# Counted loops and register arithmetic of a recurrent-plus-attention kernel written out with constant counts

## The chip, the cores and the metric

One core of one Trainium2 chip runs the kernel as one program. The metric is the device time of one execution in microseconds (us). The core has five engines that run their own instruction streams and meet at semaphores: TensorE (PE in the rows, its weight loads PEld), VectorE (DVE), ScalarE (ACT), GpSimd (POOL) and SyncE (SP), which here only issues DMAs. Each engine has a sequencer, which does register arithmetic, branches and semaphore waits and hands the rest to the engine.

## The reference, cut to what matters

```python
x = L0_attn_x                              # (16, 256, 128) float32
xn = _layernorm(x)
s = mamba_like(xn)      # W_in, two depthwise convs of 4 taps, silu; x_dbl = xs @ W_xdbl;
                        # delta = softplus(dt_low @ W_dt + 2*inv_dt); h = exp(delta*A)*h + delta*u*B (16 states);
                        # y = sum(h*C) + u*D; concat(y, z) @ W_out + b_out
g = silu(transformer(xn))
return x + s * g

# transformer: six layers of
x = attn_layer(shift_tokens(x), Wqkv, q_scale, k_scale, Wo) + x   # 16 heads of 64, q and k l2-normed,
                                                                  # rotary, causal window of 32
x = ffn_layer(shift_tokens(x), ln_g, ln_b, W1, b1, W2, b2) + x    # layer norm, a * gelu(gate) @ W2
```

## The kernel before, in words

The 16 sequences of 256 tokens form 8 groups of 512 tokens (`GT`). The kernel runs in four stages. First a layer norm of all tokens and the transposes to `xT` (channels on partitions). Then the state space stage (`state_groups`): for each of the 8 groups, 16 states; PE spreads B and C over the partitions, ACT makes the decays, DVE does the multiply and the scan (L1230, L1234), POOL weighs with C and adds (L1055, L1058).

The third and longest stage is the transformer (`flow`). Its unit of work is a turn, 48 of them with a current group. A turn carries four groups in different stages of a layer (`prev2`, `prev`, `cur`, `next`) and has 16 steps on each engine. In each step PE computes scores of a pair of heads (`scores`, L690, 16 matmul records a step), transposes probabilities (L699, L700), makes outputs (L718), and projects the next group's q and k (L335 to L337); DVE takes the maxima (L1338), multiplies by the rotary tables (L1292) and copies the transposed probabilities (L1324); ACT does the exponentials (L930); POOL normalises and rotates. The order within a step is fixed by hand-written tables. Four turns of a layer have an extra kind: in `load` and `T0` the next layer's weights are loaded and split in high and low parts and DVE makes new tables, `T1` and `T2` load the rest.

The last stage, eight small passes over the groups, takes silu on ACT (L1023), multiplies with the state space result on DVE (L1420), transposes on PE (L818) and adds x on DVE (L1424).

All engines run the same structure of loops. In `state_groups` groups 1 to 6 are a counted loop of three passes with two groups each. In `flow` the first three turns and the last ones are written with constants; between them a loop over five layers (L316) holds an inner loop `layer` of two passes with two turns each (L306) and then the four turns `load` to `T2`; the sixth layer has the inner loop alone. The last stage is a loop of eight passes. Each engine therefore takes a backward branch of L306 six times and one of L316 four times.

Where a count depends on a loop variable, the value of a wait is worked out in a register (`eng.snap`, `Bases`), `held` places the arithmetic ahead of the waits, and `settle` adds a wait on `consts_made`, a semaphore that has long been set. An instruction carries its waits itself as far as it can; other waits become semaphore instructions in front of it.

Of the kernel before, what the change touches and what calls it, by code (L numbers as in the profile page):

```python
# [19 lines left out]
GROUPS = TOKENS // GT  # L20
# [106 lines left out]
def build(nc, x_in, W_in, W_xdbl, W_dt, W_out, mvec, Wqkv, Wo, W1, W2, lvec, tabs_c, mask_c, ident_c,  # L127
          headsum_c, statepick_c, conv_w, out):
    ctx = ExitStack()
    with ctx:  # L130
# [169 lines left out]
        def flow(eng, turn, credited, plain=()):  # L300
# [15 lines left out]
            with eng.Fori(0, DEPTH - 1) as l:  # L316
                layer(l)
                for k, kind in enumerate(("load", "T0", "T1", "T2")):
                    turn(bases(eng.snap(l * GROUPS + (6 + k))), (-2, -1, 0, 1), k % 2,
# [19 lines left out]
        def after(eng, what, g, per, k):  # L339

            if not isinstance(g, int):
                eng.wait_ge(what, eng.snap(g * per + k))
            elif g * per + k > 0:
                eng.wait_ge(what, g * per + k)

        def state_groups(eng, group):

            group(0, 0, True)
            with eng.Fori(0, (GROUPS - 2) // 2) as h:
                group(eng.snap(h * 2 + 1), 1, True)  # L350
                group(eng.snap(h * 2 + 2), 0, True)
            group(GROUPS - 1, 1, False)

        def settle(eng):

            eng.wait_ge(consts_made, 1)
# [17 lines left out]
        def _(sp_e):  # L374
# [9 lines left out]
            def load_chunk(layer, c):  # L384

                done = sp_e.snap(layer * CHUNKS + (c - 1)) if not isinstance(layer, int) else layer * CHUNKS + c - 1
                if not isinstance(layer, int) or done > 0:
# [31 lines left out]
            with sp_e.Fori(0, GROUPS) as g:  # L419
# [6 lines left out]
            def turn(n, o, par, gs, kind, l):  # L426
# [3 lines left out]
                nl = l + 1 if isinstance(l, int) or kind not in ("load", "T0", "T1", "T2") else sp_e.snap(l + 1)  # L430

                def swap(j, q):

                    made = held(sp_e, n16 + (16 * q + j + 1))
# [4 lines left out]
                def keep_k_norms(h, q):  # L439

                    norms = held(sp_e, n2 + (2 * q + h + 1))
# [1058 lines left out]
```

## Time and profile before

| | us |
|---|---|
| median of 3 runs | 3862.33 (3861.29 to 3875.04) |
| profiled execution, its own time | 3852.33 |
| span of the profiled execution | 3850.5 |

The profiled execution lies 1.83 us above its span, and 10.0 us below the median of the three timed runs. It counts 107643 instructions, 31040 of them matmul records and as many weight loads. "busy" is time in which an engine works; register, branch and semaphore instructions do not count. The chain of waits is followed back from the last instruction: at each step to what released it, or to the instruction before it on its engine. "issue" in it is time in which the engine waited for nothing that the profile shows. The granted clock of TensorE is given as a share of full speed; full is 2.4 GHz and the other level, 1.2 GHz, is 0.5.

### The profile page before, as it was taken

The numbers are of one execution on the slowest core, as the hardware profiler recorded it, in microseconds if no ns is written. First come the engines' busy times: TensorE is split into PE (matmuls) and PEld (weight loads), VectorE is DVE, ScalarE is ACT, GpSimd is POOL, SyncE is SP. The second block draws the span as 40 slices with busy tenths as digits, with TensorE's granted clock in tenths as the row PEclk, the third lists the DMA queues.
The fourth block names the chain that finished last, engine by engine and source line by source line (L and its number), as shares of the span: only waits on it lengthen the run. The fifth ranks groups of instructions, "written<-read, shape, count | busy, mean of one in ns | idle before, by whom it ended". The sixth has DMA issues, their size and how long they took to land.

```text
span 3850.5 us, 107643 instructions
## 1 busy us (share of the span) xinstructions
PE 3513.4 (91%) x31040; PEld 2253.6 (59%) x31040; DVE 3251.6 (84%) x11659; ACT 3048.6 (79%) x8806; POOL 2918.7 (76%) x2417
## 2 busy tenths in 40 slices
PE   5998699999999999999999999999999999999994
PEld 2454466666666565666666666666656666666662
DVE  5778688889889888888888888888988988888882
ACT  4565588888878888888888887888877888888883
POOL 3888687778878778777788777787877877877771
PEclk9899799999999999999999999999999999999996
DMA  2000233323323233232233332333322333223222
GB/s 81 6 8 8 106 105 103 101 100 116 108 98 108 93 111 112 101 102 99 98 116 104 111 101 95 102 112 105 114 94 96 107 109 114 102 101 101 99 77 69
DMA packets 235888, 365.31 MB, mean 95 GB/s; under 512 B 43054, under 2 KB 75884, under 8 KB 235052
## 3 DMA queue, kind: packets, MB, share of 16 engines
q1 hardware_dynamic: 235276, 358.05, 27.5%
q8 instruction: 275, 4.51, 0.5%
q14 instruction: 337, 2.76, 0.2%
HBM read 125.93 MB, written 5.77 MB: 34 GB/s over the span
## 4 chain that ended last, share of the span: by engine, by line
PE 70%; DVE 14%; issue 6%; ACT 5%; POOL 2%; DMA 1%; SPq 1%; DVEq 0%; ACTq 0%; POOLq 0%
PE bank L729 9%; PE bank L335 8%; PE bank L718 8%; PE bank L690 8%; PE bank L337 7%; PE bank L336 6%; PE bank L671 5%; DVE ab L1292 4%; PE bank L699 4%; PE bank L757 4%; PE bank L700 3%; DVE sm L1338 3%; DVE pt L1324 2%; ACT L972 1%; PE bank L735 1%
## 5 line engine op out<-in xcount | busy, mean ns | idle before, releaser
L930 ACT ACTIVATE pr<-sm,nb,rq 128x128 f32<-128x128 f32 (+1 forms) x3072 | 1516.7, 500 | 22.5 <-DVE nb L1344 18.2
L1084 POOL TENSOR_TENSOR pr<-pr,rden 128x640 f32<-128x640 f32 x768 | 963.6, 1255 | 551.8 <-DVE rden L1317 550.2
L1292 DVE TENSOR_TENSOR ab<-bank,ltab 128x512 f32<-128x512 f32 x1536 | 985.5, 683 | 182.6 <-PE bank L337 161.0
L1092 POOL TENSOR_TENSOR rot<-ab,swp 128x512 f32<-128x512 f32 x768 | 984.2, 1281 | 97.7 <-DMA swp<-ab 92.0
L1338 DVE CUSTOM_DVE_ANT_0 sm<-bank,mask 128x128 f32<-128x128 f32 (+1 forms) x3072 | 840.3, 329 | 44.3 <-PE bank L690 35.3
L930 ACT ACTIVATION_READ_ACCUMULATOR pr<-sm,nb,rq 128x1 f32 x3072 | 595.3, 194 | 0.0
L690 PEld LDWEIGHTS bank<-rot 64*64 64x64 f32 x12288 | 291.0, 133 | 460.7 <-issue 460.1
L1098 POOL TENSOR_TENSOR rot<-rot,rkb 128x512 f32<-128x512 f32 x384 | 491.3, 1285 | 78.1 <-DMA rkb<-k_scratch 77.9
L1324 DVE COPY pt<-bank 128x512 f32<-128x512 f32 x768 | 531.4, 692 | 10.2
L918 ACT ACTIVATE sq<-bank 128x512 f32<-128x512 f32 x768 | 451.1, 587 | 94.8 <-DVE ab L1292 84.2
L690 PE MATMUL bank<-rot 64*64 64x96 f32 x12288 | 433.3, 256 | 87.6 <-issue 48.5
L718 PE MATMUL bank<-pt,vtok 128*64 128x160 f32 (+1 forms) x6144 | 464.1, 293 | 0.0
L699 PE MATMUL bank<-ident,pr 128*128 128x128 f32 x1536 | 399.4, 287 | 57.6 <-DVE pt L1324 55.6
L1338 DVE DVE_READ_ACCUMULATOR2_ANT bank<- 128x1 f32 x3072 | 432.2, 141 | 0.1
L939 ACT ACTIVATE wide<-bank 128x512 f32<-128x512 f32 x384 | 228.6, 595 | 247.9 <-PE bank L718 246.9
L718 PEld LDWEIGHTS bank<-pt,vtok 128*64 128x64 f32 x6144 | 370.7, 137 | 66.5 <-issue 66.1
L700 PE MATMUL bank<-ident,pr 128*128 128x128 f32 x1536 | 379.9, 274 | 0.0
L944 ACT ACTIVATE vtok<-bank 128x512 f32<-128x512 f32 x384 | 227.5, 592 | 183.6 <-PE bank L337 183.1
L729 PE MATMUL bank<-wide,wo 128*128 128x512 f32 x768 | 371.0, 606 | 0.9 <-ACT wide L939 0.9
L335 PE MATMUL bank<-xh,wqk_h 128*128 128x512 f32 x768 | 340.3, 443 | 27.0 <-ACT sq L918 25.8
L699 PEld LDWEIGHTS bank<-ident,pr 128*128 128x128 f32 x1536 | 216.4, 141 | 195.5 <-issue 156.9
L337 PE MATMUL bank<-xl,wqk_h 128*128 128x512 f32 x768 | 306.9, 400 | 0.0
(201 smaller groups left out, 6383.7 us busy)
## 6 DMA issues: line engine op xcount, KB each, us to landing
swp<-ab SPq DMA_DIRECT2D x1536, 128.0 KB, 2.0
rkb<-k_scratch SPq DMA_DIRECT2D x768, 128.0 KB, 2.9
xs<-xT SPq DMA_DIRECT2D x95, 128.0 KB, 2.3
xs<-xT SPq DMA_DIRECT2D x95, 127.5 KB, 2.4
raw<-Wqkv SPq DMA_DIRECT2D x48, 128.0 KB, 2.4
raw<-Wqkv SPq DMA_DIRECT2D x12, 256.0 KB, 2.7
wo<-Wo SPq DMA_DIRECT2D x6, 512.0 KB, 4.6
k_scratch<-rsum SPq DMA_DIRECT2D x192, 8.0 KB
```

Source lines behind the costliest of these rows:

```text
L335: eng.matmul(o, wh, ah, start=True, stop=False)
L337: return eng.matmul(o, wh, al, start=False, stop=True)
L690: mm = pe.matmul(bank[i][part, c:c + 96], rot[rows, p, c0 + 64 * half:c0 + 64 * half + 64], rot[rows, PAIRS + p, c0 + k0:c0 + k0 + 96], st ...
L699: pe.transpose(bank[2][:, 256 * i:256 * i + P], pr[:, e % 4, i, 0, 0:P], ident[:, :])
L718: mm = pe.matmul(bank[3][64 * i:64 * i + 64, cols], vtok[:, 2 * b + t, ch], pt[:, e % 4, i, t, 0:cols.stop - cols.start], start=(b == 0 an ...
L729: mm = pe.matmul(use_bank("wo", 0)[:, :], wo[:, p, :], wide[:, p, :], start=(p == 0), stop=(p == PAIRS - 1))
L930: ins = act.activation(pr[:, s % 4, i, t, 0:P + WINDOW * t], sm[:, s % 2, i, cs], ACT.Exp, bias=nb[:, s, t, i:i + 1], scale=head_scale(rq, ...
L1084: ins = pool.tensor_tensor(pr[:, e % 4, :, :, :], pr[:, e % 4, :, :, :], rden[:, e, :, :].rearrange("p t i -> p i t").unsqueeze(3) .to_bro ...
L1092: pool.tensor_tensor(rot[:, PAIRS * (j % 2) + j // 2, :], ab[:, j % 2, 0, :], swp[:, j % 2, :], ALU.add).then_inc(qk_rot, 1)
L1292: ins = dve.tensor_tensor(seqs(ab[:, j % 2, i, :]), seqs(use_bank("qk", j)[:, :]), ltab[:, 2 * (j % 2) + i:2 * (j % 2) + i + 1, :] .to_bro ...
L1324: dve.tensor_copy(pt[:, e % 4, :, :, 0:P], bank[2][:, :].rearrange("p (i t c) -> p i t c", i=2, t=2)).then_inc(p_Tsb, 1)
L1338: ins = dve.tensor_tensor_reduce(sm[:, s % 2, i, cs], bank[i][:, cs], mask[:, cs], 1.0, -3e38, ALU.add, ALU.max, mx[:, t, i:i + 1])
```

## The change

All counted loops are replaced by Python loops that write the turns, layers, groups and passes out, so every semaphore count, slice and layer number is a constant of the program. With that `held`, `settle`, the `snap` calls and all register instructions go. No engine operation of the turns and groups is changed or put in another order. The constants still form the same waits; those on `consts_made` that `settle` made are gone. PE's written program has 20272 matmul instructions where it had 5256.

```diff
-        def held(eng, n):
-
-            if not isinstance(n, int):
-                eng.to_reg(n)
-            return n
-
...
-                    self.n = {m: eng.snap(it * m + CREDIT) for m in credited}
-                    self.z = {m: eng.snap(it * m) for m in plain}
+                    self.n = {m: (it * m + CREDIT) for m in credited}
+                    self.z = {m: it * m for m in plain}
...
             def layer(l):
-                with eng.Fori(0, 2) as h:
-                    for k in range(2):
-                        g = eng.snap(h * 2 + k)
-                        it = eng.snap(h * 2 + (l * GROUPS + (2 + k)))
-                        turn(bases(it), (-2, -1, 0, 1), k, (g, eng.snap(g + 1), eng.snap(g + 4)),
-                             "first" if k == 0 else "", l)
+                for k in range(4):
+                    turn(bases(l * GROUPS + 2 + k), (-2, -1, 0, 1), k % 2, (k, k + 1, k + 4), "first" if k == 0 else "", l)
...
-            with eng.Fori(0, DEPTH - 1) as l:
+            for l in range(DEPTH - 1):
...
         def state_groups(eng, group):
 
             group(0, 0, True)
-            with eng.Fori(0, (GROUPS - 2) // 2) as h:
-                group(eng.snap(h * 2 + 1), 1, True)
-                group(eng.snap(h * 2 + 2), 0, True)
+            for g in range(1, GROUPS - 1):
+                group(g, g % 2, True)
             group(GROUPS - 1, 1, False)
-
-        def settle(eng):
-
-            eng.wait_ge(consts_made, 1)
...
                 def scores(s):
 
                     p, b = s // 2, s % 2
-                    scaled = held(pe, n8 + (p + 1))
-                    used = held(pe, n16 + s)
-                    settle(pe)
+                    scaled = (n8 + (p + 1))
+                    used = (n16 + s)
...
-            with act.Fori(0, GROUPS) as g:
+            for g in range(GROUPS):
...
                 def normalise(e, q):
-                    count = held(pool, n16 + (16 * q + e + 1))
-                    settle(pool)
+                    count = (n16 + (16 * q + e + 1))
```

The other hunks do the same in the other functions and engines.

On PE, at the end of the inner loop's second turn, this stood before (L690 are the scores that open the next turn, L335 to L337 the projections that close this one; ISA here is a fused register instruction):

```order
L335 MATMUL bank<-xh,wqk_h 128x512 [waits qk_sq]
L336 MATMUL bank<-xh,wqk_l 128x512
L337 MATMUL bank<-xl,wqk_h 128x512
L306 REGISTER_ALU
L306 COMPARE_AND_BRANCH
L279 ISA
L690 MATMUL bank<-rot 64x96 [waits sc_bias,k_norm,consts_made]
L690 MATMUL bank<-rot 64x96 x7
L625 ISA
L756 REGISTER_ALU [waits f_h]
L757 MATMUL bank<-gg,w 128x512 [waits f_h]
```

And this stands there in the changed program, where L325 to L327 are the projections, L671 the scores and L738 the down projection:

```order
L325 MATMUL bank<-xh,wqk_h 128x512 [waits qk_sq]
L326 MATMUL bank<-xh,wqk_l 128x512
L327 MATMUL bank<-xl,wqk_h 128x512
L671 MATMUL bank<-rot 64x96 [waits sc_bias,k_norm]
L671 MATMUL bank<-rot 64x96 x7
L738 MATMUL bank<-gg,w 128x512 [waits f_h]
```

The matmuls stand in the same order; the branch, the register instructions and the wait on `consts_made` between them are gone.

On ACT, in the last stage, the loop held a load of the silu table in each of its eight passes:

```order
L1022 REGISTER_ALU [waits f_add]
L1023 ISA [waits g_mul]
L1023 ACT_TABLE_LOAD
L1023 ACTIVATE ab<-xT 128x512
L1020 REGISTER_ALU
L1020 COMPARE_AND_BRANCH
```

Written out, the same place is:

```order
L1002 ACT_TABLE_LOAD [waits g_mul]
L1002 ACTIVATE ab<-xT 128x512 [waits f_add]
L1002 ACTIVATE ab<-xT 128x512 [waits g_mul,f_add] x7
```

The table is loaded once, and the other seven passes have the silu alone.

## Rows read from the trace of the kernel before

**Rows 1.** The page, busy time: us, share of the span, instructions

```profile
PE 3513.4 (91%) x31040; PEld 2253.6 (59%) x31040; DVE 3251.6 (84%) x11659; ACT 3048.6 (79%) x8806; POOL 2918.7 (76%) x2417
```

**Rows 2.** The page, TensorE's granted clock in tenths, 40 slices

```profile
PEclk9899799999999999999999999999999999999996
```

**Rows 3.** The page, chain that ended last, by engine

```profile
PE 70%; DVE 14%; issue 6%; ACT 5%; POOL 2%; DMA 1%; SPq 1%; DVEq 0%; ACTq 0%; POOLq 0%
```

**Rows 4.** Timeline of PE, scores that open turns: start, us, what [idle before]

```profile
560.00 0.54 PE L690 MATMUL bank<-rot 64*64 64x96 f32 x13
...
628.39 0.56 PE L690 MATMUL bank<-rot 64*64 64x96 f32 x16
...
699.85 0.69 PE L690 MATMUL bank<-rot 64*64 64x96 f32 x16 [3.02 <-issue]
...
770.12 0.56 PE L690 MATMUL bank<-rot 64*64 64x96 f32 x16
...
838.50 0.56 PE L690 MATMUL bank<-rot 64*64 64x96 f32 x16
...
909.05 0.56 PE L690 MATMUL bank<-rot 64*64 64x96 f32 x16 [0.39 <-DVE nb L1344]
...
979.33 0.56 PE L690 MATMUL bank<-rot 64*64 64x96 f32 x16
...
3641.32 0.56 PE L690 MATMUL bank<-rot 64*64 64x96 f32 x16
...
3709.86 0.56 PE L690 MATMUL bank<-rot 64*64 64x96 f32 x16
```

**Rows 5.** Chain in order of time, its long pieces of issue: start, us

```profile
696.84 3.02 issue
...
1676.72 3.58 issue
...
2381.72 2.92 issue
...
3499.69 2.98 issue
```

**Rows 6.** Sequencer instructions of L306 on PE: count, ns min/median/max, first and last start

```profile
L306 PEldq COMPARE_BRANCH  x12: 78/1694/3664, 696.0 to 3640.5; - x12
```

**Rows 7.** Timeline of DVE at the first backward branch of L306

```profile
695.47 0.16 DVE L1344 TENSOR_TENSOR nb<-bank,nrq 128x4 f32<-128x4 f32 x1
698.64 0.18 DVE L1317 RECIPROCAL rden<-den 128x4 f32<-128x4 f32 x1 [3.01 <-ACT pr L930]
```

**Rows 8.** Windows: stretch, length, busy of PE, PEld, DVE, ACT, POOL, clock, DMA

```profile
699.80:703.20 3.40, 3.35 (x22) 1.82 (x22) 3.21 (x13) 0.60 (x1) 1.64 (x2) 0.55 0.23 83
703.20:706.60 3.40, 3.40 (x36) 1.85 (x39) 1.88 (x4) 1.93 (x7) 3.32 (x3) 0.95 0.01 4
```

**Rows 9.** Windows of two groups of the state space stage

```profile
141.60:182.40 40.80, 37.18 (x105) 20.31 (x105) 31.54 (x36) 24.94 (x42) 32.74 (x27) 0.92 0.02 7
...
303.50:341.30 37.80, 34.19 (x106) 18.73 (x105) 31.30 (x35) 24.95 (x42) 32.86 (x27) 1.00 0.02 7
```

**Rows 10.** Timeline of one pass of the last stage

```profile
3831.14 1.28 ACT L1023 ACT_TABLE_LOAD   x1 [0.98 <-DVE ab L1420]
...
3831.17 1.11 PE L818 MATMUL bank<-ident,ab 128*128 128x128 f32 x4 [1.79 <-DVE ab L1420]
3832.42 0.69 DVE L1424 TENSOR_TENSOR rot<-rot,bank 128x512 f32 x1 [1.39 <-PE bank L818]
3832.44 0.63 ACT L1023 ACTIVATE ab<-xT 128x512 f32 x1
3833.23 0.69 DVE L1420 TENSOR_TENSOR ab<-ab,rot 128x512 f32<-128x512 f32 x1
```

**Rows 11.** The page, queues that fetch instructions: packets, MB, share

```profile
q8 instruction: 275, 4.51, 0.5%
q14 instruction: 337, 2.76, 0.2%
```

More of the change, by code:

```diff
@@ L339, in after @@
         def after(eng, what, g, per, k):
-            if not isinstance(g, int):
-                eng.wait_ge(what, eng.snap(g * per + k))
-            elif g * per + k > 0:
+            if g * per + k > 0:
                 eng.wait_ge(what, g * per + k)
@@ L429, in turn @@
                 nk, n2, n8, n16 = n.z[64], n.n[2], n.n[8], n.n[16]
-                nl = l + 1 if isinstance(l, int) or kind not in ("load", "T0", "T1", "T2") else sp_e.snap(l + 1)
+                nl = l + 1
                 def swap(j, q):
-                    made = held(sp_e, n16 + (16 * q + j + 1))
+                    made = (n16 + (16 * q + j + 1))
                     sp_e.wait_ge(qk_mul, made)
@@ L505, in _ @@
             ov = out.rearrange("b (t p) c -> p (b t) c", p=P)
-            with sp_e.Fori(0, GROUPS) as g:
+            for g in range(GROUPS):
                 sp_e.wait_ge(g_out, g + 1 + CREDIT)
@@ L573, in group @@
             def group(g, par, more):
-                before = g - 1 if isinstance(g, int) else pe.snap(g - 1)
-                following = g + 1 if isinstance(g, int) else pe.snap(g + 1)
-                if isinstance(g, int) and g == 0:
+                before = g - 1
+                following = g + 1
+                if g == 0:
                     spread_B(0, g, par)
@@ L812, in _ @@
             flow(pe, turn, (1, 2, 3, 4, 8, 16), (32,))
-            with pe.Fori(0, GROUPS) as g:
+            for g in range(GROUPS):
                 pe.wait_ge(g_mul, g + 1 + CREDIT)
@@ L874, in split_high @@
                 due = {0: 32, 2: 64, 4: 96, 6: 112, 1: 32, 3: 48, 5: 64, 7: 80}[c]
[L875 to L876 removed]
+                landed = total * layer + due
                 act.wait_ge(raw_in[c % 2], landed)
@@ L962, in split_high_x @@
                 def split_high_x(buf):
-                    landed = held(act, n.z[32] + 64 if cur is not None else n.z[32] + 32)
-                    settle(act)
+                    landed = (n.z[32] + 64 if cur is not None else n.z[32] + 32)
                     act.wait_ge(xs2_in, landed)
@@ L1018, in _ @@
             flow(act, turn, (1, 2, 3, 4, 8, 16), (32,))
-            with act.Fori(0, GROUPS) as g:
+            for g in range(GROUPS):
                 act.wait_ge(f_add, DEPTH * GROUPS + CREDIT)
@@ L1031, in split_low @@
             def split_low(layer, c):
-                made = held(pool, layer * CHUNKS + c + 1 if isinstance(layer, int) else pool.snap(layer * CHUNKS + (c + 1)))
-                settle(pool)
+                made = layer * CHUNKS + c + 1
                 pool.wait_ge(w_hi, made)
@@ L1101, in normed @@
                 def normed(q):
-                    ready = held(pool, n1 + (q + 1))
-                    vectors = held(pool, l + 2) if kind == "T2" else None
-                    settle(pool)
+                    ready = (n1 + (q + 1))
+                    vectors = (l + 2) if kind == "T2" else None
                     if vectors is not None:
@@ L1115, in split_low_x @@
                 def split_low_x(buf):
-                    made = held(pool, n1 + 3 if cur is not None else n1 + 2)
-                    settle(pool)
+                    made = (n1 + 3 if cur is not None else n1 + 2)
                     pool.wait_ge(x_hi, made)
@@ L1256, in layer_tables @@
                 ins.then_inc(lvq_ok, 1)
-                made = held(dve, base + 2)
-                settle(dve)
+                made = (base + 2)
                 dve.wait_ge(lvq_ok, made)
@@ L1329, in maxima @@
                     p, b = s // 2, s % 2
-                    scores = held(dve, n16 + (s + 1))
-                    used = held(dve, n16 + (s - 1 if s >= 2 or prev is not None else 0))
-                    settle(dve)
+                    scores = (n16 + (s + 1))
+                    used = (n16 + (s - 1 if s >= 2 or prev is not None else 0))
                     dve.wait_ge(sc_ps, scores)
@@ L1416, in _ @@
             dve.wait_ge(s_in, 32)
-            with dve.Fori(0, GROUPS) as g:
+            for g in range(GROUPS):
                 dve.wait_ge(g_silu, g + 1)
```

62 lines of the change are left out of this document (28 added, 34 removed).

## The prediction, made before the changed kernel ran

> **What bounds the kernel now.** I read the page first. PE works in 91% of the span, DVE in 84%, ACT in 79% [rows 1]; TensorE's clock is full in nearly all of the transformer [rows 2]; and the chain of waits is PE for 70%, DVE for 14%, with 6% of "issue" [rows 3]. So the transformer is bound by PE, with short pieces where DVE or ACT is late. What sequencers do counts only where it stops PE.
>
> To see that, the next view is the timeline of PE, cut at the scores that open each turn [rows 4]. A turn is a repeated unit with the same work, so its length is the measure. The turn from 560.00 lasts 68.39 us, the next, which ends with the inner loop's backward branch, 71.46 (699.85 minus 628.39), the one after it 70.27, and the next again 68.38. The row that opens the turn at 699.85 has 3.02 us of idle time put down to "issue": nothing that the profile shows was missing. The load turn lasts 70.55 and T0 70.28. The turn from 3641.32 is written with constants already in this kernel and is a full turn but for the load of a shifted input; it lasts 68.54.
>
> Then the chain in order of time. Its pieces of issue over 2.5 us in the transformer's loops are ten, of which four stand in [rows 5]; the smallest is 2.92, and all ten add up to 31.6. Ten is also the number of backward branches taken on each engine: six of L306, four of L316. The branch instruction itself takes between 78 ns and 3.66 us on PE [rows 6]. DVE shows the same hole at the same place, 695.63 to 698.64 [rows 7]. It is put down to ACT's exponentials there, but for each engine it is the start of the loop body again.
>
> After the hole the clock: 0.55 for the 3.4 us from 699.80, 0.95 in the next 3.4 [rows 8]. PE was idle for 3.0 us, then the chip granted it the lower level for 3.4 us, and this is what makes the following turn 70.27 where the undisturbed one is 68.38.
>
> **The change, part by part.** *Backward branches of the transformer.* Ten holes of 2.92 to 3.58 us go [rows 5]: 31.6 us. All engines have theirs within a few us of each other and wait for the same semaphores, so it is one hole a branch, not five. What is late next is PE itself: a turn that ends without a taken branch, such as the one from 560.00, goes on without a gap into the next [rows 4].
>
> *Clock after them.* Each restart at the lower clock costs up to 70.27 - 68.38 = 1.89 us [rows 4]. Ten of them would be 18.9; none is the lower bound, since the change does not say that the clock stays up. I can check the sum by the turns. The 44 turns from 560.00 to 3641.32 last 3081.3. If 34 turns take 68.39 and five pairs of load and T0 take 140.83 each (979.33 minus 838.50), that is 2325.3 + 704.2 = 3029.5, or 51.8 less. The later pairs may be longer than the first, and then this is too much. Between 31.6 and 51.8 I take 48: it is nearest to what the turns say, and it means 16.4 us for the clock.
>
> Here the Trainium skill bears on the case. Runtime: NRT & Kernel Launch, section Instruction fetch mechanics, says that prefetch is sequential and that a taken branch to a place outside two pages forces a fetch before execution goes on. The 3.0 us holes agree with it. The Trainium skill's page Advanced Engine Details and Errata, section Control Flow Timing, gives a compare-and-branch some 108 ns; by that figure the ten branches would be worth 1.1 us together (an estimate of that page), and this case's holes of 3.02 and 3.58 us say otherwise.
>
> *Register arithmetic, `held` and `settle` in the ordinary turns.* I cost this at nothing. The cover is that sequencers work ahead while their engines are busy. The test is the turn from 3641.32: it has no register arithmetic and lasts 68.54, against 68.39 with it [rows 4]. It still has the waits on `consts_made`, so those are unproved. Upper bound: 0.5 us a turn, about the 0.39 that PE waits for DVE at the scores at 909.05 [rows 4], or 22 for 44 turns; lower bound: the 0.15 between these two turns the other way, a loss of 7. I take 0, nearest to the constant turn.
>
> *Load and T0 turns.* They are 2.16 and 1.89 us longer than an ordinary one [rows 4], 20 us for five pairs. Most of it must be the work itself (splits on ACT and POOL, tables on DVE), which stays; a part is register work for slices and counts. Between 0 and 10 us I take 1.
>
> *State space stage.* It too has a loop with two backward branches. The group 141.60 to 182.40 lasts 40.8 at a mean clock of 0.92, the one from 303.50, in the same loop, 37.8 at 1.00 [rows 9]. So what differs between groups is the clock, 3.0 us a group; the four groups from 141.60 to 303.50 have a mean of 40.5. The change doesn't touch what precedes the clock's fall there, but shifts of a fraction of a us may move it. Between a loss of 6 and a gain of 13 I take 0.
>
> *Last stage.* A pass takes 2.89 us: silu's table load at 3831.14 (1.28), silu (0.63), the product at 3833.23 (0.69) and two short hand-overs. The load goes in seven passes, but 7 x 1.28 = 9.0 is not the gain. Beside it runs product, PE, sum, product: PE starts at 3831.17, the sum at 3832.42, it takes 0.69, and the next product starts at 3833.23 [rows 10]. That is 2.06 from PE's start to the product, 0.12 after the end of the sum, and with the product's 0.69 and the hand-over to PE again about 2.88. It becomes the bound in the load's place. It has three register instructions on its path of about 0.05 each: 0.1 to 0.2 a pass, 1 us for seven. If that cover weren't there, it would be 9.
>
> *Instruction fetch.* The new program is straight. The two queues moved 4.51 + 2.76 = 7.27 MB [rows 11], which over 107643 instructions is 67.5 bytes each, so already before every executed instruction is fetched about once per execution, loops or not. Without register instructions it should be slightly less. Cost 0, since the turns between two branches show no hole.
>
> Sum: 48 + 0 + 1 + 0 + 1 + 0 = 50. The profiled execution would go from 3852.3 to 3802; the median of the timed runs lies 10.0 higher, so 3862.3 - 50 = 3812.
>
> **Rivals.**
> 1. *More than the branches.* If waits on `consts_made` and register work are exposed after all, and the state space stage keeps its clock, the further gain is about 11 for ordinary turns (half of the 22), 5 in load and T0, and 9 of the 13: 25 together, 3787. For it: DVE and POOL have many such instructions. Against it: the constant turn is no faster.
> 2. *Holes go, clock does not.* PE loses time elsewhere at the lower level, or an engine that caught up in the hole is now late. Then only 31.6 + 1 goes, 3830. For it: the clock also fell in the state space stage, without a branch [rows 9]. Against it: turns that follow an unbranched end show nothing of the kind.
> 3. *No change.* The stall is not the branch but something at that point of the layer, such as queued DMAs. Then 1 or 2 us, 3861. Against it: the fall-through after the inner loop's second pass has no hole, at the same work (770.12 to 838.50 is 68.38).
> 4. *Slower: straight code outruns its fetch.* PE's queue brought 275 packets in the span, one in 14 us [rows 11]. If the next packet isn't always asked for ahead in a program of this length, PE stops for a hole of 3.1 us plus 1.9 at the low clock, 5.0 for each. It eats the gain at 10 such stops and makes the kernel slower by over 0.5% (19.3 us) from 14 on; one stop in ten packets would be 25, or 125 us: 3862 - 50 + 125 = 3937. For it: nothing in this trace is straight for longer than eight turns. Against it: within those turns dozens of packets pass without one hole.
>
> **How the numbers follow.** The forecast has 0.70, rival 1 0.12, rival 2 0.10, rival 3 0.04, rival 4 0.04. The time is the forecast's, 3812. The range takes in rivals 1 and 2 and the bounds of the state space stage beyond them by a little: 3785 to 3838; rivals 3 and 4 stay outside. A measurement of this kernel can tell about 0.5%, 19.3 us, from no change. Faster by more than that: the forecast and rivals 1 and 2, 0.92; within it rival 3 and a quarter of rival 4, 0.05; slower the rest of rival 4, 0.03.
>
> **What would show it.** Right: no piece of issue over 2.5 us in the chain between two turns; a granted clock of 1.00 through the transformer; every turn but load and T0 at 68.4, with no rise in those after the former branches; fetch queues of 6 to 7 MB; one load of silu's table in the last stage at a pass of 2.7 to 2.9 us. Wrong: turns of 68.4 that became 67.9 or less (rival 1); new holes between steps at regular distances in PE's timeline (rival 4); holes of 3 us that stayed at the ends of turns (rival 3); slices of the clock under 1.00 in the transformer (rival 2).

## The result, and the profile after

The changed kernel takes 3804.16 us, the median of 4 runs (3802.19 to 3806.15). The kernel before took 3861.81 (3854.6 to 3875.04, 4 runs) beside it. The ratio is 0.9847 [0.982, 0.9874], its 95% interval in brackets. From profiled execution to profiled execution it is 3852.33 to 3804.09, so 48.2 us less, where the prediction's sum had 50. From median to median it is 57.7 less; why the two differ is taken up at the end of the account of the prediction.

The page of the kernel after:

```profile
PE 3507.6 (92%) x31040; PEld 2251.6 (59%) x31040; DVE 3255.1 (86%) x11659; ACT 3030.9 (80%) x8799; POOL 2918.3 (77%) x2417
...
PEclk9899799999999999999999999999999999999997
...
q8 instruction: 250, 4.10, 0.5%
q14 instruction: 247, 2.02, 0.2%
...
PE 58%; DVE 18%; POOL 8%; issue 8%; ACT 5%; DMA 2%; SPq 1%; DVEq 0%; POOLq 0%; ACTq 0%
```

TensorE's busy time is nearly what it was [rows 1]; the shares rose because the span shrank. The chain has more of DVE and POOL in it than [rows 3]: with the holes gone, these two are what is late next. The fetch queues moved 6.12 MB in place of 7.27 [rows 11].

The timeline of PE, cut at the scores that open each turn, is the answer to [rows 4]:

```profile
567.33 0.56 PE L671 MATMUL bank<-rot 64*64 64x96 f32 x16
...
635.58 0.56 PE L671 MATMUL bank<-rot 64*64 64x96 f32 x16
...
703.81 0.56 PE L671 MATMUL bank<-rot 64*64 64x96 f32 x16
...
772.03 0.56 PE L671 MATMUL bank<-rot 64*64 64x96 f32 x16
...
840.26 0.56 PE L671 MATMUL bank<-rot 64*64 64x96 f32 x16
...
912.39 0.56 PE L671 MATMUL bank<-rot 64*64 64x96 f32 x16 [0.39 <-DVE nb L1316]
...
981.54 0.56 PE L671 MATMUL bank<-rot 64*64 64x96 f32 x16
```

The first four turns are 68.25, 68.23, 68.22 and 68.23 long; before, the second and third were 71.46 and 70.27. No turn of this kernel begins with a gap put down to issue. The load turn, 840.26 to 912.39, is longer than before: 72.13 against 70.55.

By stretches of the span the 48.2 us split like this:

| stretch | before | after | difference |
|---|---|---|---|
| start to third full turn (constants, state space, first turns) | 560.0 | 567.3 | +7.3 |
| 44 turns up to turn 46 | 3081.3 | 3030.8 | -50.5 |
| the last two turns and the last stage | 209.2 | 204.2 | -5.0 |

**What remains in the load turns.** The chain's three longest pieces of "issue" in the transformer, start and us:

```profile
904.75 4.44 issue
...
2557.68 4.43 issue
...
3110.18 4.41 issue
```

They are no holes of a branch. At each of them VectorE is inside one instruction, the scaling of a rotary table. The line's own view, ns min/median/max:

```profile
L1228 DVE TENSOR_SCALAR ltab<-tab,lvq x24: 340/398/4696, 387.8 to 3120.4; 128x256 f32<-128x256 f32 x24
```

Before, its longest took 1.37 us. The timelines of DVE and of POOL around 904.75 show what lies beside it:

```profile
904.57 4.96 DVE L1228 TENSOR_SCALAR ltab<-tab,lvq 128x256 f32<-128x256 f32 x2
909.57 0.75 DVE L1329 SCALAR_TENSOR_TENSOR gg<-bank,lv,gg 128x512 f32<-128x512 f32 x1
```

```profile
902.90 1.29 POOL L1015 TENSOR_TENSOR wqk_l<-raw,wqk_h 128x512 fp32r<-128x512 f32 x1
904.13 2.54 POOL L1075 TENSOR_TENSOR rot<-rot,rkb 128x512 f32<-128x512 f32 x2
906.62 1.27 POOL L1061 TENSOR_TENSOR pr<-pr,rden 128x640 f32<-128x640 f32 x1
907.83 1.28 POOL L1069 TENSOR_TENSOR rot<-ab,swp 128x512 f32<-128x512 f32 x1
```

GpSimd works from 902.90 to 909.11 without a pause, five instructions back to back, and the first of the two scalings ends 0.16 us after the last of these. The same is seen in three of five load turns. PE then stops for 2.2 us and gets the lower clock for 3.4 us twice out of three.

In the kernel before, the first scaling stood at the same place of the same row of GpSimd's:

```profile
903.70 0.97 DVE L1254 TENSOR_SCALAR ltab<-tab,lvq 128x256 f32<-128x256 f32 x1
```

```profile
903.24 1.28 POOL L1098 TENSOR_TENSOR rot<-rot,rkb 128x512 f32<-128x512 f32 x1
```

It ended 0.15 us after this instruction, although the next of GpSimd's followed without a pause. So the end of one instruction can be enough; in the long cases VectorE did not get its turn at three such ends.

The clock also falls once after a 2.00 us gap that is GpSimd's (rotary sum, L1075). The row with the gap, and the windows at and behind the fall (columns as in [rows 8]):

```profile
1246.35 0.68 PE L671 MATMUL bank<-rot 64*64 64x96 f32 x16 [2.00 <-POOL rot L1075]
```

```profile
1246.70:1250.10 3.40, 3.40 (x32) 2.42 (x23) 2.35 (x12) 2.94 (x4) 3.40 (x4) 0.50 0.42 154
1250.10:1253.50 3.40, 3.40 (x18) 2.22 (x20) 1.71 (x3) 2.38 (x3) 3.40 (x3) 1.00 0.00 1
```

Three such stretches of 3.4 us are all that is left in the transformer's 44 turns; before there were eight, one of them twice as long.

**The last stage.** One pass in the kernel after, all engines:

```profile
3782.73 1.12 PE L799 MATMUL bank<-ident,ab 128*128 128x128 f32 x4 [1.38 <-DVE ab L1392]
3782.77 0.63 ACT L1002 ACTIVATE ab<-xT 128x512 f32<-128x512 f32 x1 [1.87 <-DVE ab L1392]
3783.88 0.69 DVE L1396 TENSOR_TENSOR rot<-rot,bank 128x512 f32<-128x512 f32 x1 [1.21 <-PE bank L799]
3784.49 0.69 DVE L1392 TENSOR_TENSOR ab<-ab,rot 128x512 f32<-128x512 f32 x1
...
3785.23 1.12 PE L799 MATMUL bank<-ident,ab 128*128 128x128 f32 x4 [1.38 <-DVE ab L1392]
```

A pass is 2.50 us (3785.23 minus 3782.73) where it was 2.90, and the product starts 0.61 after the sum where it was 0.81 [rows 10].

### The profile page after: what moved, and what is told of

Its sections match the earlier page's. It is cut to its first block, busy times and chain, and to the rows that moved or that the text cites. A ratio compares the mean times of both kernels' runs of the same rounds, so it can differ in the third digit from the quotient of the medians.

```text
span 3802.3 us, 95850 instructions
## 1 busy us (share of the span) xinstructions
PE 3507.6 (92%) x31040; PEld 2251.6 (59%) x31040; DVE 3255.1 (86%) x11659; ACT 3030.9 (80%) x8799; POOL 2918.3 (77%) x2417
## 4 chain that ended last, share of the span: by engine, by line
PE 58%; DVE 18%; POOL 8%; issue 8%; ACT 5%; DMA 2%; SPq 1%; DVEq 0%; POOLq 0%; ACTq 0%
PE bank L710 8%; PE bank L699 7%; PE bank L325 6%; DVE ab L1265 6%; PE bank L671 5%; PE bank L327 5%; PE bank L326 5%; PE bank L653 4%; PE bank L738 4%; DVE sm L1310 4%; PE bank L680 3%; POOL rot L1069 3%; POOL pr L1061 3%; PE bank L681 2%; DVE pt L1297 2%
## 5 line engine op out<-in xcount | busy, mean ns | idle before, releaser
L671 PEld LDWEIGHTS bank<-rot 64*64 64x64 f32 x12288 | 288.2, 132 | 430.9 <-issue 353.3
L1297 DVE COPY pt<-bank 128x512 f32<-128x512 f32 x768 | 531.4, 692 | 10.2
L1075 POOL TENSOR_TENSOR rot<-rot,rkb 128x512 f32<-128x512 f32 x384 | 491.6, 1286 | 63.2 <-DMA rkb<-k_scratch 62.6
L671 PE MATMUL bank<-rot 64*64 64x96 f32 x12288 | 432.0, 256 | 57.0 <-DVE nb L1316 34.1
L325 PE MATMUL bank<-xh,wqk_h 128*128 128x512 f32 x768 | 339.4, 442 | 26.3 <-ACT sq L898 25.2
L327 PE MATMUL bank<-xl,wqk_h 128*128 128x512 f32 x768 | 307.3, 400 | 0.0
```

The source lines that it names most:

```text
L325: eng.matmul(o, wh, ah, start=True, stop=False)
L327: return eng.matmul(o, wh, al, start=False, stop=True)
L671: mm = pe.matmul(bank[i][part, c:c + 96], rot[rows, p, c0 + 64 * half:c0 + 64 * half + 64], rot[rows, PAIRS + p, c0 + k0:c0 + k0 + 96], st ...
L1297: dve.tensor_copy(pt[:, e % 4, :, :, 0:P], bank[2][:, :].rearrange("p (i t c) -> p i t c", i=2, t=2)).then_inc(p_Tsb, 1)
```

## The experiments

All kernels below are one text in which each engine's control flow is chosen by a switch, so that loops, registers and waits can be put back for one engine or one stage. Times are medians; the ratio is to the kernel before on the same chip. "44 turns" is the stretch of 3030.8 above.

**No backward branch.** Every pass of the transformer's two loops stands in a counted loop of one pass. In the text of the kernel the counts stay in registers; `held` and `settle` stay, and so do the loops of the state space and last stages.

```diff
-                with eng.Fori(0, 2) as h:
-                    one_pass(l, h)
+                for i in range(2):
+                    with once(eng, i) as h:      # eng.Fori(0, 1), h = i in a register
+                        one_pass(l, h)
```

> The kernel before, with each pass of the transformer's loops written out but wrapped in a counted loop of one pass: all register arithmetic, held and settle stay, only the ten backward branches are never taken. Theory A (the backward branches and the slow clock behind them are the gain): the 44 turns fall from 3081 to about 3031 us, no 3 us hole at ends of turns, median about 3810 (3800 to 3818). Theory B (register arithmetic is what costs): within 10 us of the kernel before, about 3855. Theory C (any jump costs, forward ones too): holes stay, since each pass is entered by a jump, and there are 15 of them; 3862 or more.

3808.27 (3806.1 to 3810.76), 0.9861 [0.9844, 0.9877]. 44 turns: 3030.8, no gap of issue over 1.2 us, most ordinary turns 68.23 to 68.25. PE's timeline at the turns that began with a hole and a slow clock before:

```profile
633.42 0.56 PE L750 MATMUL bank<-rot 64*64 64x96 f32 x16
...
701.66 0.56 PE L750 MATMUL bank<-rot 64*64 64x96 f32 x16
...
769.90 0.56 PE L750 MATMUL bank<-rot 64*64 64x96 f32 x16
```

That is the whole gain of the turns. But this run is not the control that it was meant to be. The trace counts 98312 instructions, against 107643 before and 95850 in the changed kernel, and within an ordinary turn it has no more than 3 register instructions on an engine, where the kernel before has 32 to 64. The counts of a loop of one pass became constants in the built program. So this run took away the branches and the register work together, and can't tell them apart. The next runs can: they keep the register work, on all engines or on one.

**The outer loop alone stays.**

```diff
-                with eng.Fori(0, 2) as h:
-                    one_pass(l, h)
+                for h in range(2):
+                    one_pass(l, h)
```

> The kernel before with only the inner loop of two passes (L306) written out; the loop over five layers stays, so four backward branches of ten are left. Theory A: six holes of about 3.1 us and their slow clock go, 6 x 4.8 = 29 us, median about 3833, and four holes of 2.9 to 3.6 us stay in PE's timeline, one a layer. Theory B (it is the register arithmetic): 3855 or more, since layer and counts are still worked out in registers.

3834.69 (3825.22 to 3837.04), 0.992 [0.9902, 0.9939]. 44 turns: 3060.5. The register work is there, 27 to 62 instructions an engine in an ordinary turn of the loop. The six holes of the inner loop are gone all the same, and four gaps of 2.90 to 3.44 us are left, one for each backward branch. So the holes belong to the branches, not to the register work. PE's timeline at the first:

```profile
1119.44 0.56 PE L750 MATMUL bank<-rot 64*64 64x96 f32 x16 [3.44 <-issue]
```

The turn that ends with the first branch is 71.91 and the next 70.01, where 68.40 is an undisturbed one: 5.1 us lost, and 5.8, 5.7 and 6.3 at the other three. Undisturbed turns are 68.39 to 68.41 in the loop. In the last layer, which is constant, the shortest is 68.24.

**One engine at a time.** Loops and register work on the engine named, constants on all others. All of these but ScalarE's have the waits on `consts_made` back on all engines; a run below shows that these cost nothing.

```diff
-FLOW = {'rest': 'const'}
+FLOW = {'rest': 'const', 'PE': 'loops'}      # then ACT; SP and POOL; DVE
```

> The changed kernel, but TensorE alone keeps the transformer's loops and its register arithmetic (the waits on consts_made are there again on all engines). Theory A says that the engines' holes lie beside each other and that each branch costs one hole: then TensorE's ten holes alone cost nearly all of the 48 us, 3850. Rival: the holes of the engines add up or the longest chain goes over ScalarE's, which starts 5 us later: then TensorE alone costs half, 3825 to 3835.

3856.12 (3848.35 to 3862.97), 0.9984 [0.9973, 0.9994]. 44 turns: 3085.6, with ten gaps; the first in PE's timeline:

```profile
706.28 0.56 PE L750 MATMUL bank<-rot 64*64 64x96 f32 x16 [3.27 <-issue]
```

TensorE's loops alone bring back all of the loss in the turns: (3085.6 - 3030.8) / 10 = 5.5 us a branch. Its 60 register instructions a turn cost nothing: undisturbed turns are 68.23 to 68.25.

> The changed kernel, but ScalarE alone keeps the transformer's loops and its register arithmetic. TensorE and VectorE have no holes of their own. Theory A: ScalarE works beside the bound; its ten holes of about 2.7 us reach TensorE only in part, 0 to 1.5 us each, 3804 to 3820. Rival (any engine's hole stops all, since they wait for each other in each step): 2.7 us plus the slow clock for each, 3845 or more.

3806.05 (3803.19 to 3808.97), 0.9855 [0.9839, 0.9872]; 44 turns: 3030.2. ACT has its holes (2.4 to 2.9 us between its sequencer's records), and they cost nothing, nor do its 61 register instructions a turn.

> The changed kernel, but SyncE and GpSimd keep the transformer's loops and register arithmetic (and the waits on consts_made are back on all engines). Their inner loop's body is 198 and 226 instructions, and its branch showed a hole of under 0.3 us before; the outer one's 827 and 929, with holes of 2.4 to 2.6 us. Theory A (a hole depends on the length of the body, and those of engines with idle time are covered): median 3804 (3800 to 3810), no hole on TensorE. Rival (SyncE's and GpSimd's outer holes reach TensorE, since the swaps and rotations feed it in each step): four times 2.5 us and the slow clock, 3815 to 3822.

3806.78 (3805.86 to 3808.22), 0.9863 [0.9847, 0.9878]; 44 turns: 3034.2. SyncE's and GpSimd's holes, 2.4 to 2.8 us at the outer loop's branches (0.2 to 0.3 at the inner one's), show no stop of PE either.

> The changed kernel, but VectorE alone keeps the transformer's loops and its register arithmetic (the waits on consts_made are back on all engines). Two questions. First, does its hole reach TensorE? VectorE is busy 86% of the span and TensorE waits for it in most steps. Theory A (one hole a branch, whichever of the two has it): ten holes of 2.8 us reach TensorE nearly whole, with a slow clock behind them, the turns from 2 to 45 go from 3031 to 3065 to 3080, median 3838 to 3853. Rival (only TensorE's own branch counts, VectorE catches up): 3804 to 3815. Second, ordinary turns were 68.39 before and 68.23 since; loops on TensorE, ScalarE or GpSimd with SyncE did not bring the 0.16 back. If it is VectorE's loop, turns are 68.39 here; if not, 68.23.

3874.19 (3866.66 to 3876.23), 1.0021 [1.0011, 1.003]; 44 turns: 3101.8. My expectation was wrong: VectorE's loops alone are slower than everybody's together. Nine times PE stands 3.6 to 3.9 us for VectorE's copy of the transposed probabilities (1.4 at the tenth), and the lower clock then lasts 6.8 us. The timelines of DVE and PE at the first branch:

```profile
703.31 0.18 DVE L1391 RECIPROCAL rden<-den 128x4 f32<-128x4 f32 x1 [3.03 <-ACT pr L997]
705.64 0.24 DVE L1397 STREAM_TRANSPOSE pt<-pr 32x64 f32<-32x64 f32 x1 [2.15 <-issue]
```

```profile
706.73 0.45 PE L759 MATMUL bank<-ident,pr 128*128 128x128 f32 x1 [3.69 <-DVE pt L1398]
```

There are two holes, not one. The sequencer's records have them at the same place of the program each time, whether the branch went to the inner head or to the outer one, two instructions before it. Both heads lie just ahead of that place.

**The same, moved on by 12 instructions.**

```diff
             if how in ("loops", "outer"):
+                for _ in range(24):
+                    eng.wait_ge(consts_made, 1)
                 with eng.Fori(0, DEPTH - 1) as l:
```

> The run with loops on VectorE alone once more, with 24 waits that are long met (12 instructions) ahead of VectorE's outer loop, so that all that follows lies 12 instructions further on. In the run without them nine of ten backward branches show two holes on VectorE: 2.7 to 3.0 us right behind the branch and 2.0 to 2.4 us a few instructions later, always at the same place of the program (ahead of L1394), whether the branch went to the inner head or to the outer one three instructions before it; the tenth, in the last layer's copy of the loop, shows one hole, and its next turn took 70.6 us where the others took 74.6 to 75.4. Theory A, the second hole belongs to where the loop's head lies: just ahead of a place at which the fetch has to begin anew. Moved 12 instructions on, the head lies behind that place, each branch has one hole of 2.7 to 3.0, the turn behind it takes 70.5 to 71.5, the nine branches lose 4 to 4.5 less each, 36 to 40 us together: about 3836, ratio about 0.992 to 0.993. Rival B, the second hole belongs to the branch itself when the other engines run on (their reads are in its way), wherever the head lies: nine or ten double holes stay, 3874, ratio 1.002. Rival C, the second holes go but the others wait as long, since it is the first that stops them: double holes gone, turns still 74 to 75, 3870.

3833.76 (3830.13 to 3844.31), 0.9933 [0.9917, 0.9949]; 44 turns: 3057.0. As theory A had it, there are ten branches, ten single holes, none doubled. What lies at that place of the program, no trace shows; that the fetch begins anew there stays an argument. DVE and PE at the first:

```profile
704.41 0.18 DVE L1393 RECIPROCAL rden<-den 128x4 f32<-128x4 f32 x1 [3.01 <-ACT pr L999]
704.62 0.24 DVE L1399 STREAM_TRANSPOSE pt<-pr 32x64 f32<-32x64 f32 x1
```

```profile
705.71 0.30 PE L761 MATMUL bank<-ident,pr 128*128 128x128 f32 x1 [1.56 <-DVE pt L1400]
```

PE's gaps are now 1.54 to 1.71 us and the clock falls behind none of them. Nine second holes were worth 3101.8 - 3057.0 = 44.8, so 5.0 each: 2.1 of standing, and the rest I put down to the clock.

**The tables written as another instruction.**

```diff
-                    ins = dve.tensor_scalar(ltab[:, i, :], tab[:, i, :], lvq[:, part:part + 1], KUP if part else 1.0,
-                                            ALU.mult, ALU.mult)
+                    ins = dve.scalar_tensor_tensor(ltab[:, i, :], tab[:, i, :], KUP if part else 1.0,
+                                                   lvq[:, part:part + 1].to_broadcast([P, SEQ]), ALU.mult, ALU.mult)
```

> The changed kernel with the four table instructions of a layer on VectorE written as scalar_tensor_tensor (table times constant, times the layer's scale spread over the columns) in the place of tensor_scalar; same result, same place. In the changed kernel's trace three of the first ones took 4.69 us and all others that stood beside GpSimd's work 1.0 to 1.4, each ending 0.15 us after an instruction of GpSimd; the undisturbed ones take 0.34. Theory A (tensor_scalar on VectorE can't start while GpSimd's instructions follow each other closely, and loses several of them; scalar_tensor_tensor isn't held): all take about 0.45 us, no step of 6 us at the end of load turns, load turns at about 69.0 in the place of 71.0, median 3795 (3792 to 3799). Theory B (the tables wait for something else, a semaphore or SBUF access): the long ones stay, 3804.

3806.73 (3802.72 to 3809.98), 0.9852 [0.9833, 0.9871]. The view of the line:

```profile
L1328 DVE SCALAR_TENSOR_TENSOR ltab<-tab,lvq x24: 409/425/4845, 390.2 to 3124.2; 128x256 f32<-128x256 f32 x24
```

Four of five are held as long, so theory A was wrong: this form doesn't escape either. The Trainium skill (SBUF — State Buffer, section Who interferes with whom) has both VectorE's 2-port modes and its instructions with two SBUF inputs contend with GpSimd for one pair of ports; this run agrees for the second kind with 4.8 us. The same page lets the loser wait until the other's instruction ends. In the kernel after, the table passed the ends of three of GpSimd's (905.4, 906.7, 907.9) and came in at the fourth, 909.1, where GpSimd paused. In the kernel before it came in at the first of them. So the page's rule gives the least wait, and in this kernel the loser can lose again.

**The tables at another time.** The first half's tables are made in T0, in front of the second half's, and no longer in the load turn's last step.

```diff
-                        if s == 15 and kind == "load":
-                            layer_tables(nl, 0)
...
                         if kind == "T0":
+                            layer_tables(nl, 0)
                             layer_tables(nl, 1)
```

> The changed kernel with the next layer's two q tables made one step later: at T0's step 0, right ahead of the two k tables, in the place of the load turn's last step. Same instructions, tensor_scalar. In the load turn's last step GpSimd has four instructions in a row, and the first table waited 4.7 us beside them in three of five layers of the changed kernel; at T0's step 0 GpSimd is idle from 914.9 to 917.5. Theory A (VectorE's instruction waits for a gap of GpSimd's): no table over 1.5 us, load turns 72 to 69, T0 turns up to 0.8 longer, the turns from 2 to 45 fall from 3030.7 to about 3020, median about 3794 (3789 to 3800). Theory B (the long tables come from elsewhere, such as the loads of weights): they stay long at the new place, 3804 or more.

3792.4 (3789.44 to 3795.22), 0.9827 [0.9814, 0.9841] to the kernel before. It is the fastest of all. The line's view:

```profile
L1328 DVE TENSOR_SCALAR ltab<-tab,lvq x24: 339/351/1109, 386.2 to 3106.8; 128x256 f32<-128x256 f32 x24
```

44 turns: 3018.4, so 12.4 less than the kernel after; load turns 68.75 to 69.70, and no stretch of the lower clock in the 44 turns. So it is the table's place, behind GpSimd's row of instructions, that cost this time.

**The other parts of the change put back.** Each with the rest as in the kernel after.

```diff
-STATE_LOOP, LAST_LOOP, SETTLE = False, False, False
+STATE_LOOP, LAST_LOOP, SETTLE = True, False, False
```

> The changed kernel with the state space stage (and SyncE's storing of its results) in loops and registers again; the rest constant. In the changed kernel this stage ended 7.3 us later than before, with the slow clock in all seven later groups against five before. Theory A (chance of the clock: its falls lie on a grid that isn't tied to the program's start): the stage ends anywhere between 372 and 380 us, median within 4 us of the changed kernel's 3804. Theory B (writing the stage out made it slower): the stage ends at 372 to 374 and the median falls to 3797.

3803.73 (3794.81 to 3809.99), 0.9843 [0.9819, 0.9868]; the state space stage's last scan ends at 379.5, as in the kernel after (379.6) and not as before (372.3). So the loop there isn't what made the stage later.

```diff
+STATE_LOOP, LAST_LOOP, SETTLE = False, False, True
```

> The changed kernel with the waits on consts_made back in all places where settle made them. Theory A (a wait on a semaphore that is long set is hidden): ordinary turns stay at 68.23 us, median 3804 (3801 to 3807). Theory B (these waits are the 0.16 us by which an ordinary turn became shorter, 68.39 to 68.23): turns of 68.39, 44 x 0.16 = 7 us more, 3811.

3803.19 (3793.47 to 3807.58), 0.9844 [0.9819, 0.987]; ordinary turns 68.23. The waits on `consts_made` cost nothing.

```diff
+STATE_LOOP, LAST_LOOP, SETTLE = False, True, False
-                act.activation(ab[:, 0, 0, :], xT[:, bass.ds(g * GT, GT)], ACT.Silu).then_inc(g_silu, 1)
+                act.activation(ab[:, 0, 0, :], xT[:, bass.ds(g * GT, GT)], ACT.Copy).then_inc(g_silu, 1)
```

> The changed kernel with the last stage as a loop of eight passes with registers again, and a plain copy in the place of silu there, so that no table is loaded in a pass; what is left out is silu in the last stage. A pass took 2.90 us before and takes 2.50 now. Theory A (the prediction's: the loaded table hides beside TensorE's transposes, the register instructions are on the path): passes of 2.8 to 2.9 us. Theory B (the table load was the bound): 2.50 to 2.6.

3807.93 in one run, which leaves out silu in the last stage. The copy takes as long as silu did, 0.63 us. The last stage's products on DVE, and a sum between them:

```profile
3784.42 0.69 DVE L1494 TENSOR_TENSOR ab<-ab,rot 128x512 f32<-128x512 f32 x1
...
3786.50 0.69 DVE L1498 TENSOR_TENSOR rot<-rot,bank 128x512 f32 x1 [1.39 <-PE bank L878]
3787.10 0.68 DVE L1494 TENSOR_TENSOR ab<-ab,rot 128x512 f32<-128x512 f32 x1
```

A pass is 2.68 us: of the 0.40 that a pass got shorter, the table load had 0.22 and loop and registers 0.18. Both theories had expected one of the two to have it all. The product starts 0.60 after the sum's start, as in the kernel after, with the register instructions still there.

## Why the prediction came out, step by step

**Backward branches and the clock behind them: 48 predicted.** The ten holes of [rows 5] are gone, and the run with the outer loop alone ties them to the branches: six went with six branches and four stayed with four, under the same register work. The 44 turns gave 50.5. In it are 5.4 of the next point (34 turns by 0.16) and 3.3 of the load and T0 turns, and the five turns behind T0 lost 2.9 (343.1 to 345.2, beside their 0.8 of the 0.16). That leaves 45: 31.6 for the holes as predicted, and 13 for the clock and the restart where I had 16.4. The clock had not fallen behind all ten before, only in eight stretches.

"One hole a branch, not five" was right in the sum and too simple as a mechanism. By the 44 turns, PE's loops alone cost 5.5 a branch, VectorE's alone 2.1 (moved on; 3057.0 less 3030.8 less 5.4, by ten) or 6.6 (nine of ten doubled), the other engines' nothing. All at once cost 4.5 for the ten of the kernel before, and 5.1 to 6.3 at each of the four of the outer loop. So the holes of all engines together cost about what PE's alone do: they overlap. Whether 5.5 against 4.5 is more than the chance of the clock's falls (twelve against eight in the two traces), no run shows.

**Ordinary turns: 0 predicted, 0.16 us each found. This step of the prediction was wrong.** [rows 4] has 68.38 to 68.39; after has 68.23. I had put register arithmetic at nothing, with the cover that sequencers work ahead while their engines are busy. On VectorE there is a place where they can't. The difference sits in one step (step 10: 3.54 before, 3.38 after), in which PE waits for VectorE's copy of probabilities (L1324, now L1297). That copy is late because VectorE's clamp of the row sums (`clamp`, L1351) starts late. PE's sum and the clamp before, and the same pair after:

```profile
599.34 1.07 PE L671 MATMUL bank<-sq,headsum 128*32 128x512 f32 x8
600.64 0.69 DVE L1351 TENSOR_SCALAR rsum<-bank 128x512 f32<-128x512 f32 x1 [0.64 <-PE bank L671]
```

```profile
674.92 1.07 PE L653 MATMUL bank<-sq,headsum 128*32 128x512 f32 x8
676.06 0.69 DVE L1323 TENSOR_SCALAR rsum<-bank 128x512 f32<-128x512 f32 x1 [0.56 <-PE bank L653]
```

From the start of PE's sum to the clamp it is 1.30 us before and 1.14 after. Between the two stands an instruction of VectorE's sequencer that works out the value of the clamp's second wait, behind its first wait, which is the one for PE. The view of its line in the kernel before:

```profile
L1349 DVEq ALU_OP  x44: 40/40/40, 600.5 to 3613.4; - x44
```

It begins only when PE's signal is there, and a semaphore instruction follows it; then comes the clamp. In the kernel after, the clamp starts where that arithmetic did. In all traces, but for a few single turns, step 10 follows this instruction. With register work on VectorE it is 3.54 (before, the outer loop, VectorE alone, twice); without, it is 3.38, whatever the other engines do. Within one run it changes too: with the outer loop alone it is 3.54 in the 40 turns of the loop and 3.38 in the five behind it. The run of loops of one pass has 3.38 because it has no such arithmetic.

The turn from 3641.32, on which the prediction rested its zero, was a bad witness. It has no such arithmetic, and its clamp starts early; but VectorE then stands for 0.1 us within its row maxima, put down to issue, and step 10 is 3.60 all the same. Why it stands there, no run shows.

**Load and T0 turns: 1 predicted.** Found: 2.8 longer in load turns, 6.0 shorter in T0. What I had not on my list is a VectorE instruction that is held behind GpSimd, and it is what made load turns longer. The kernels with the tables in their old place show it in three to five of five load turns, those with loops on all or one of the engines among them; the kernel before shows it in none, though the table meets the same row of GpSimd's at the same point. So it isn't the missing holes that bring it, and why the kernel before escapes stays open. Register work seems to have a part in T0: the five T0 turns add up to 350.4 to 351.4 us in the kernels with it on VectorE, and 346.7 to 348.5 in those without it but the one with loops on SyncE and GpSimd (350.5). Before they were 354.2; how the 6.0 divides isn't shown.

**State space: 0 predicted, 7.3 lost.** In the kernel after the clock falls in seven groups, before in five, at 3.0 us a group [rows 9]. The loop put back changes nothing. Nine of the twelve other kernels end the last scan between 376.0 and 379.5, the others at 375.3, 380.3 and 382.0; before, at 372.3, is the lowest of all. So the 7.3 may be the luck of one profiled execution of the kernel before. The bound (a loss of 6) was passed by 1.3. That a given kernel always has the same number of falls was not tried.

**Last stage: 1 predicted, 5.0 with the last two turns.** Seven passes by 0.40 are 2.8; turn 46 gave 0.3 and the last turn 1.5 (55.02 to 53.51). The 0.18 a pass of loop and registers is what I had (0.1 to 0.2). The step that failed is the cover of the table load. I took the sum as what the product waits for. [rows 10] says otherwise: the product starts at 3833.23, silu ends at 3833.07, the sum at 3833.11, and both are late, silu by the table load. After, the product starts 0.61 behind the sum's start, before the sum's recorded 0.69 is over. So the 0.12 us between the sum and the product was silu's hand-over, not VectorE's; with the table load alone taken out, the product starts 0.60 behind the sum's start.

**Fetch: 0 predicted, 0 found.** 497 packets and 6.12 MB for 95850 instructions are 63.8 bytes each, and no stop of PE over 1.2 us in the turns of the straight kernels is put down to issue. Rival 4 is out; the doubled hole is the nearest to what it described, and it came only behind a branch. (One stop in ten of its 275 packets would be 27 or 28, not the 25 that it reckons with; nothing hangs on it.)

**Rivals 1 to 3.** Rival 3 is out by the first two experiments. Rival 2's mechanism showed in three stretches of the lower clock, 3.4 us each, and rival 1's in the 0.16 us and the last stage; they nearly cancel each other. The sum of 50 was right within 2 us of the profiles' difference, but by terms that were off and cancel, and that is luck: clock -3, ordinary turns +5.4, load and T0 +2.3, the turns behind T0 -2.9, state space -7.3, last stage +4.0.

**The 10.0 us added to the profile.** Median against median the gain is 57.7, not 48.2, and the forecast of 3812 was 8 too high. I had taken the 10.0 us between the profiled execution and the median as a constant of the kernel. It was not. The 52 timed runs of the kernel before beside the experiments, on four chips, take 3854.6 to 3872.4, the median 3862.8, with mean granted clocks of 0.971 to 0.976, the median 0.973. The profiled execution, 3852.33 at 0.977, is faster than all of them and has the highest clock. A straight line through the 52 gives 2.5 us for each 0.001 of the clock, so 0.004 would be 10 us (an estimate from these runs). The changed kernel's timed runs are at 0.976 to 0.978 and its profiled one at 0.977. So the profile before was of an execution with an unusually high clock, which was luck, and the two profiles understate the gain. In which stages the others had the lower clock, no trace shows. The kernels without a taken branch in the transformer all have medians between 3792.4 and 3808.3.

**Signs named beforehand.** No piece of issue at a turn's end: so it was. Turns of 68.4: 68.23, less by the register arithmetic and far from the 67.9 of rival 1. A clock of 1.00 throughout: all but three stretches. Queues of 6 to 7 MB: 6.12. A pass of 2.7 to 2.9: 2.50, wrong.

## What to carry to other kernels

A backward branch over a long body costs a hole of about 3 us on each engine that takes it, but only what the bounding engine sees counts: write the loop out where PE, or the engine PE waits for, branches, and leave it on the others if the program's size matters. If a loop must stay, look at the sequencer's records for a second hole a few instructions behind the head; in the one case tried, some instructions of padding ahead of the loop took it away. Register arithmetic is free while it is worked out ahead of the waits. Behind a wait that ends late it is not: 0.16 us a turn here. When you put a feature back to test it, count in the trace whether it is really back. And when stalls go, look again at what now runs side by side: here 12 us more came from moving a few small VectorE instructions away from a row of GpSimd's.

## What the runs showed of the hardware

- The hole goes with the length of the body. Behind backward branches over 6 to 227 of their own instructions, SyncE, GpSimd, ACT and VectorE show 0.11 to 0.29 us between the sequencer's records (loops of the state space and last stages, and the inner loop on SyncE and GpSimd); over 514 and more it is 2.4 to 3.2 us. On PE the branch instruction itself lasts that long: 0.2 to 0.35 us over 8 and 279 instructions (weight loads not counted), 3.3 to 3.9 over 1464 and more. A branch that isn't taken is followed by the next record after 0.03 to 0.06. No body between 279 and 514 was measured.
- The hole can come twice on VectorE: 2.7 to 3.0 us and 2.0 to 2.4 us more at a fixed place of the program, in the run where the loop's head lies just ahead of it; 12 instructions further on, all ten holes are single.
- One register instruction (40 ns) behind a wait that ends late, with the semaphore instruction after it, put VectorE's next instruction 0.16 us later (1.30 against 1.14 us).
- In the 44 turns of all fourteen traces, PE stood for 1.2 to 1.8 us 40 times without a fall of the clock behind it. Of 49 stops of 2.0 to 2.5 us, 29 had one, of 3.4 us each; of 24 stops of 2.9 to 3.7 us at branches, 21, of 3.4 or 6.8 us; of nine of 3.6 to 3.9 us in the middle of a turn, all nine, of 6.8 us. No fall came without such a stop.
- VectorE's table instruction of 0.34 us, one or two inputs in SBUF, was held for 4.6 to 4.85 us behind GpSimd instructions that follow each other without a pause, past the ends of three. In the kernel before it met the same row and came in at the first end, after 0.97 to 1.00 us in all. Which of the two happens, no run explains.
